# Causal short attention in a decoder kernel: first keys ahead of the row transposes, copies divided anew, a second pair of banks for the first maxima

## The reference

```python
q = (queries @ Wq.T + bq).reshape(N, L, H, -1)
k = (keys @ Wk.T + bk).reshape(N, S, H, -1)
v = (values @ Wv.T + bv).reshape(N, S, H, -1)
sm = jnp.einsum('nlhd,nshd->nlhs', q, k) / math.sqrt(D)
sm = jnp.where(triu(ones((L, S)), k=1)[None, :, None, :], -jnp.inf, sm)
attn = jnp.einsum('nlhs,nshd->nlhd', softmax(sm), v)
return attn.reshape(N, L, H * D) @ Wo.T + bo
```

## Time and profile before

| | us |
|---|---|
| median of 3 runs | 1110.2 (1110.14 to 1110.24) |
| span of the profiled execution | 1106.3 |
| time of the profiled execution beside its span | not listed; the runs' median lies 3.9 above it |
| PE busy in the span | 899.7 (81%) |
| VectorE busy | 741.0 (67%) |
| ScalarE busy | 583.1 (53%) |
| GpSimd busy | 242.7 (22%) |
| causal attention stage, first PE instruction to that of the next stage | 456.5 to 543.6 |

### The profile page before, as it was taken

How to read it: one execution, slowest core, us unless ns; L and a number is a source line. 1 busy time by engine, 2 the same in 40 slices (tenths; PEclk the granted TensorE clock), 3 DMA queues, 4 the chain that set the end, 5 groups by cost and what they waited for, 6 DMA issues and landing times. The chain is left out here.

```text
span 1106.3 us, 18228 instructions
## 1 busy us (share of the span) xinstructions
PE 899.7 (81%) x6163; PEld 555.5 (50%) x6163; DVE 741.0 (67%) x2036; ACT 583.1 (53%) x1770; POOL 242.7 (22%) x356
## 2 busy tenths in 40 slices
PE   6997999999795462679766799794777999999997
PEld 3446999998463130425543377373672233333333
DVE  6568777877573896446576644623557888898863
ACT  5785777777323200413454434452353777777784
POOL 4004455554100113202120000322501111111110
PEclk9599999999897685658876899796795899999999
DMA  9600000000004500000001000562122011111000
GB/s 231 153 19 1 2 1 2 2 1 2 1 1 57 62 0 15 16 0 2 1 1 54 1 1 1 165 170 56 21 41 67 1 27 27 27 27 21 2 1 15
DMA packets 76185, 35.81 MB, mean 32 GB/s; under 512 B 35236, under 2 KB 74572, under 8 KB 76093
## 3 DMA queue, kind: packets, MB, share of 16 engines
q1 hardware_dynamic: 73724, 33.61, 13.7%
q0 software_dynamic: 896, 0.63, 0.2%
q10 hardware_dynamic: 1472, 0.41, 0.2%
HBM read 24.42 MB, written 11.05 MB: 32 GB/s over the span
## 5 line engine op out<-in xcount | busy, mean ns | idle before, releaser
L493 DVE TENSOR_REDUCE L3x_NMP<-L3x_pM 128x1 f32<-128x361 f32 x384 | 178.2, 524 | 20.0 <-PE L3x_pM L726 19.2
L647 ACT ACTIVATE L3x_E<-L3x_pS 128x400 f32<-128x400 f32 (+1 forms) x375 | 164.5, 509 | 47.3 <-PE L3x_pS L750 46.3
L726 PE MATMUL L3x_pM<-ctx_tm 64*128 64x361 bf16 x384 | 103.6, 340 | 14.0 <-DVE L3x_NMP L493 9.7
L750 PE MATMUL L3x_pS<-ctx_tm 64*128 64x400 bf16 (+1 forms) x375 | 105.5, 350 | 1.6 <-POOL ctx_tm L437 1.2
L1787 ACT ACTIVATE L0x_E<-L0x_E,ctx_r 128x100 f32<-128x100 f32 x288 | 105.1, 369 | 0.5 <-DVE L0x_E L1667 0.5
L767 PE MATMUL L3x_pO<-L3x_E,CT 128*32 128x400 f32 (+1 forms) x768 | 85.1, 515 | 0.6 <-ACT L3x_E L647 0.4
L726 PEld LDWEIGHTS L3x_pM<-ctx_tm 64*128 64x128 bf16 x384 | 30.2, 96 | 109.5 <-DVE L3x_NMP L493 90.4
L1913 PE MATMUL L0x_pU<-ctx_tm,L0x_E 128*100 128x129 f32 x576 | 67.8, 273 | 1.1 <-POOL L0x_E L1596 1.1
L1596 POOL TENSOR_TENSOR L0x_E<-L0x_E,L0x_RZ 128x1200 f32<-128x1200 f32 x24 | 52.6, 2193 | 72.3 <-DVE L0x_RZ L1692 72.3
L1901 PE MATMUL L0x_pS<-L0x_QS,CT 128*128 128x100 f32 x576 | 68.4, 275 | 0.0
L1901 PEld LDWEIGHTS L0x_pS<-L0x_QS,CT 128*128 128x128 f32 x576 | 66.2, 192 | 0.4 <-ACT L0x_QS L1779 0.4
(11 more groups left out here) (681 smaller groups left out, 2120.6 us busy)
## 6 DMA issues: line engine op xcount, KB each, us to landing
ctx_tm<-in_ctx SPq DMA_DIRECT2D x8, 704.0 KB
ctx_tm<-key_terms SPq DMA_DIRECT2D x16, 270.8 KB, 4.3
key_terms<-ctx_tm SPq DMA_DIRECT2D x42, 90.2 KB
ctx_tm<-in_L_ffn_wi SPq DMA_DIRECT2D x4, 512.0 KB, 7.5
ctx_tm<-in_L_ffn_wo SPq DMA_DIRECT2D x4, 512.0 KB
ctx_tm<-query_terms SPq DMA_DIRECT2D x16, 75.0 KB, 3.6
slots_in<-L2a_zeros SPq DMA_DIRECT2D x8, 129.0 KB
L2f_XS<-slots_in SPq DMA_DIRECT2D x4, 258.0 KB, 3.0
```

Source lines behind the costliest of these rows:

```text
L493: nc.vector.tensor_reduce(NMP[:, p, i // NC4, a, i % NC4:i % NC4 + 1], v, AX.X, ALU.max, negate=True).then_inc(s_mr, 1)
L647: nc.scalar.activation(E[0:r, n % EB, :], score_bank(n)[0:r, 0:NG * T], ACT.Exp, scale=SCALE8).then_inc(s_e, 1)
L726: nc.tensor.matmul(pM[:, n % 3, 0:CW], key_rows(QS, a)[:, b, p, 128 * x:128 * x + 128], key_rows(KS, a)[:, b % KB, c, p, :], start=True, s ...
L750: nc.tensor.matmul(score_bank(n)[0:NW[k], 0:NG * T], key_rows(KS, a)[:, b % KB, k % 4, p, 128 * (k // 4):128 * (k // 4) + NW[k]], key_rows ...
```

## The change

- PE's start: the key product of the first half goes ahead of `ln_tensor`; then come the transposes, the first half's query product and the second half's key product. The value products move behind `max_scores(0)` and the second half's query product behind `max_scores(1)`.
- Copies: the first half's four masked key copies go from ACT to DVE (`keys_by_vector`); the first half's plain query copy and all five of the second half go from DVE to ACT (`queries`), masked with a second table of masked biases, bgq, which POOL makes.
- Banks: units 2, 4 and 6 put their maxima's scores into pO instead of pM (`max_banks`); units 2 to 7 wait for one reduction less (`reader_before`). Unit 2 waits for the values to be read out of pO, `weigh(0)` for seven reductions.
- Two semaphores, s_kv and s_qa, count the moved copies. The non-causal call keeps its order.

```diff
-def ln_tensor(nc, pe, m, q, banks, src=None):
+def ln_tensor(nc, pe, m, q, banks, src=None, rows=range(B)):
 
     src = m.XN if src is None else src
-    for b in range(B):
+    for b in rows:
...
+            bgq = s.sb("bgq", [128, NG])
...
+        if causal:
+            s_kv, s_qa = s.sem("keys_by_vector"), s.sem("queries_by_scalar")
...
+        BY_ACT = 0 if causal else NG
...
+        def in_out_banks(u):
+            return causal and u in (2, 4, 6)
+
+        def max_banks(u):
+            return pO if in_out_banks(u) else pM
+
+        def reader_before(u):
+            if in_out_banks(u):
+                return u - 1
+            return u - 1 if causal and 3 <= u <= 7 else u
...
+                    nc.gpsimd.tensor_tensor(bgq[:, :], m.gmask[:, :], bias[0][:, 0:1].broadcast_to((128, NG)),
...
                 def query(h, i):
                     if i == 0:
                         dve.wait_ge(s_q, h + 1)
+                    elif causal:
+                        dve.wait_ge(s_qa, 1)
...
-                    if i == 0 and causal:
-                        nc.vector.tensor_scalar(QN[:, c], src, bias[0][:, 0:1], None, ALU.add).then_inc(s_qs, 1)
-                    elif i == 0:
+                    if i == 0:
...
+                def keys_by_vector():
+                    dve.wait_ge(s_bg, 1)
+                    dve.wait_ge(s_k, 1)
+                    for g in range(BY_ACT, NG):
+                        nc.vector.tensor_scalar(KB[:, g, 0:HALF], pX[:, 0:HALF], m.gmask[:, g:g + 1], bg[:, g:g + 1],
+                                                ALU.mult, ALU.add).then_inc(s_kv, 1)
...
-                                            pM[0:T, :, 0:NG * T].rearrange("t a (g k) -> t a g k", k=T),
+                                            max_banks(u)[0:T, :, 0:NG * T].rearrange("t a (g k) -> t a g k", k=T),
...
-                for i in range(NQ):
+                if causal:
+                    keys_by_vector()
+                for i in range(1 if causal else 0, NQ):
                     query(0, i)
...
-                        for i in range(NQ):
-                            query(1, i)
+                        if not causal:
+                            for i in range(NQ):
+                                query(1, i)
...
+                def queries(h, lo, hi):
+                    act.wait_ge(s_q, h + 1)
+                    c, src = slice(h * HALF, (h + 1) * HALF), pS[:, h, 0:HALF]
+                    for i in range(lo, hi):
+                        if i == 0:
+                            nc.scalar.activation(QN[:, c], src, ACT.Identity, bias=bias[0][:, 0:1]).then_inc(s_qa, 1)
+                        else:
+                            nc.scalar.activation(QB[:, i - 1, c], src, ACT.Identity, bias=bgq[:, i - 1:i],
+                                                 scale=m.gmask[:, i - 1:i]).then_inc(s_qa, 1)
...
-                    for g in range(NG):
+                    for g in range(BY_ACT if h == 0 else NG):
...
+                    if causal and h == 0:
+                        act.wait_ge(s_kv, NG)
...
+                if causal:
+                    queries(0, 0, 1)
                 key(0)
                 key(1)
+                if causal:
+                    queries(1, 0, NQ)
...
+                def key_product(h):
+                    if causal:
+                        pe.wait_ge(s_cxs, h + 1)
+                    else:
+                        pe.wait_ge(q.xTs, h + 1)
+                    nc.tensor.matmul((pX, pP)[h][:, 0:HALF], wT[:, 1, :],
+                                     (CX if causal else m.XNT)[:, h * HALF:(h + 1) * HALF],
+                                     start=True, stop=True).then_inc(s_k, 1)
+
+                def query_product_of(h):
+                    pe.wait_ge(q.xTs, h + 1)
+                    nc.tensor.matmul(pS[:, h, 0:HALF], wT[:, 0, :], m.XNT[:, h * HALF:(h + 1) * HALF],
+                                     start=True, stop=True).then_inc(s_q, 1)
+
+                def value_products():
+                    for b in range(B):
+                        src = (CX if causal else m.XNT)[:, b * T:(b + 1) * T]
+                        out = pO[0:T, b // HB, (b % HB) * D:(b % HB + 1) * D] if causal \
+                            else pO[0:T, 0, b * KD:(b + 1) * KD]
+                        last = nc.tensor.matmul(out, src, wT[:, 2, 0:KD], start=True, stop=True)
+                    last.then_inc(s_v, 1)
...
+                    pe.wait_ge(s_w, 1)
+                    key_product(0)
+                    ln_tensor(nc, pe, m, q, [pS[:, 0, :], pS[:, 1, :]])
+                    query_product_of(0)
+                    key_product(1)
+                else:
+                    ln_tensor(nc, pe, m, q, [pS[:, 0, :], pS[:, 1, :]])
+                    pe.wait_ge(s_w, 1)
+                    query_product_of(0)
+                    key_product(0)
+                    key_product(1)
+                    query_product_of(1)
+                    value_products()
...
                     b, p = u // 2, u % 2
+                    bank = max_banks(u)
                     if u == 0:
-                        pe.wait_ge(s_ks, NG)
-                        pe.wait_ge(s_qs, 1)
+                        if causal:
+                            pe.wait_ge(s_kv, NG)
+                            pe.wait_ge(s_qa, 1)
+                        else:
+                            pe.wait_ge(s_ks, NG)
+                            pe.wait_ge(s_qs, 1)
                     elif u == 2 * HB:
-                        pe.wait_ge(s_ks, NQ + NG)
-                        pe.wait_ge(s_qs, NQ + 1)
+                        pe.wait_ge(s_ks, BY_ACT + 1 + NG)
+                        if causal:
+                            pe.wait_ge(s_qa, 2)
+                        else:
+                            pe.wait_ge(s_qs, NQ + 1)
+                    if u == 2 and causal:
+                        pe.wait_ge(s_vs, 1)
                     if u >= 1:
-                        pe.wait_ge(s_mr, u)
+                        pe.wait_ge(s_mr, reader_before(u))
...
-                            nc.tensor.matmul(pM[0:T, a, 0:NG * T], m.ident16[0:T, 0:T], mask16[:, 0, :],
+                            nc.tensor.matmul(bank[0:T, a, 0:NG * T], m.ident16[0:T, 0:T], mask16[:, 0, :],
...
-                        nc.tensor.matmul(pM[0:T, a, 0:NG * T], group_rows(QN, j)[:, tokens(b)],
+                        nc.tensor.matmul(bank[0:T, a, 0:NG * T], group_rows(QN, j)[:, tokens(b)],
...
-                        pe.wait_ge(s_ks, NQ)
+                        pe.wait_ge(s_ks, BY_ACT + 1)
...
-                        pe.wait_ge(s_qs, 2 * NQ)
-                        pe.wait_ge(s_ks, 2 * NQ)
+                        pe.wait_ge(s_qs, NG if causal else 2 * NQ)
+                        if causal:
+                            pe.wait_ge(s_qa, 1 + NQ)
+                        pe.wait_ge(s_ks, BY_ACT + NG + 2)
...
                     if b == 0:
                         pe.wait_ge(s_vs, 1)
+                        if causal:
+                            pe.wait_ge(s_mr, 7)
...
+                    if causal and t == 0:
+                        value_products()
+                    if causal and t == 1:
+                        query_product_of(1)
```

More of the change, by code:

```diff
@@ L988, in _ @@
                     nc.gpsimd.tensor_tensor(bg[:, :], m.gmask[:, :], bias[1][:, 0:1].broadcast_to((128, NG)),
+                                            ALU.mult)
+                    nc.gpsimd.tensor_tensor(bgq[:, :], m.gmask[:, :], bias[0][:, 0:1].broadcast_to((128, NG)),
                                             ALU.mult).then_inc(s_bg, 1)
@@ L1308, in _ @@
                             last.then_inc(s_cx, 1)
-                ln_tensor(nc, pe, m, q, [pS[:, 0, :], pS[:, 1, :]])
-                pe.wait_ge(s_w, 1)
-                if causal:
-                    pe.wait_ge(s_cxs, 2)
-                    nc.tensor.matmul(pX[:, 0:HALF], wT[:, 1, :], CX[:, 0:HALF], start=True, stop=True)\
-                      .then_inc(s_k, 1)
-                    nc.tensor.matmul(pP[:, 0:HALF], wT[:, 1, :], CX[:, HALF:TOK], start=True, stop=True)\
-                      .then_inc(s_k, 1)
@@ L1317, in _ @@
-                pe.wait_ge(q.xTs, 1)
-                nc.tensor.matmul(pS[:, 0, 0:HALF], wT[:, 0, :], m.XNT[:, 0:HALF], start=True, stop=True)\
-                  .then_inc(s_q, 1)
-                if not causal:
-                    nc.tensor.matmul(pX[:, 0:HALF], wT[:, 1, :], m.XNT[:, 0:HALF], start=True, stop=True)\
-                      .then_inc(s_k, 1)
-                pe.wait_ge(q.xTs, 2)
-                if not causal:
-                    nc.tensor.matmul(pP[:, 0:HALF], wT[:, 1, :], m.XNT[:, HALF:TOK], start=True, stop=True)\
-                      .then_inc(s_k, 1)
@@ L1327, in _ @@
-                nc.tensor.matmul(pS[:, 1, 0:HALF], wT[:, 0, :], m.XNT[:, HALF:TOK], start=True, stop=True)\
-                  .then_inc(s_q, 1)
-                for b in range(B):
```

(6 more changed lines are left out.)

## The result

The changed kernel takes **1093.9 us** (median of 4 runs, 1092.19 to 1095.93) against 1110.2 of the kernel before: ratio 0.9861, 95% interval 0.9844 to 0.9877. It is faster, as forecast. The time is 3.4 us above the predicted 1090.5 and inside the range of 1087 to 1098.

A forecast was written before the change was run, and what follows sets the result against it. It took an alternating chain in the causal stage, no engine full, at half clock for 34.1 us, as the bound. 19.5 + 0.3 less 0.1 turns span 1106.3 into 1086.6; plus 3.9 gives 1090.5 us, range 1087 to 1098.

The forecast's parts named there:

- Step 1: Causal stage's start: key product ahead of the transposes, four masked key copies on DVE, 2.49 us, done at 463.3.
- Step 2: Eight row transposes queue behind the key product: 1.4 us taken, bounds 0.95 and 2.22; ACT's plain query copy ends 464.2.
- Step 3: First products of the causal stage: first reduction starts at 466.7 instead of 468.46, 1.8 us gained.
- Steps 4 and 5: Query copies leave DVE, second bank pair for ticks 1 to 7: 4.5 us gained at reduction 1, 8.6 at reduction 3.
- Step 6: Scores and exponentials bind next: exponential 0 at 475.6, exponential 4 at 485.0; 19.5 us gained, between 17.3 and 20.7.
- Step 7: Rest of the causal stage: same instructions at full clock, about 0.3 us less; added waits cost 0.1.
- The clock: PE's granted clock stays 1.00 throughout steps 5 and 6; forecast with later stages within 3 us, chance 0.72.
- The first rival: Clock falls anyway near 471 in the causal stage: gain 9.9 us, time 1100.3, or 1094 to 1102; chance 0.14.
- the second rival: Stages behind the causal one give back 4 to 8 us through shifted low-clock stretches: 1094 to 1098; chance 0.09.
- the term of 3.9: Whole program: median of the runs, 1110.2, lies 3.9 us above the profiled span, added to the predicted span of 1086.6.
- clock stays down to the end: Clock doesn't rise again in the causal stage, so the kernel is slower than before: 1115 us; chance 0.03.
- chain not shortened: ACT's five query copies make score 0 late and first ticks only queue: 1108 to 1111 us; chance 0.02.

The follow-up runs named there:

- the three delays: Changed kernel with two, four or eight extra copies out of PSUM at the end of DVE's causal-stage work: 1090.2, 1090.8 and 1093.9 us.
- the idle products two stages on: Changed kernel plus twelve unread 128 x 128 PE products in the fixed-keys stage, two stages behind the causal one: 1088.6 us.
- the three with a part undone: Changed kernel with one pair of banks, PE's old start order, or the old division of copies, one at a time: 1099.6, 1099.1 and 1098.7 us.
- The repeated kernel: Changed kernel, nothing edited, timed again in more runs: 1090.1 us, ratio 0.9817 to the kernel before.
- the kernel with idle products: Kernel before the change plus unread 128 x 400 PE products behind ticks 1 to 8 of the causal stage: 1100.4 us.

## Why the prediction was right, and where it wasn't

The stage began 0.4 us sooner than in the kernel before (456.13 for 456.51), so a step that took just what was said stands 0.4 earlier than its predicted time.

- **Step 1**, keys by DVE from 460.8 and 2.49 long: 460.36 and 2.50. Right; nothing else wanted DVE.
- **Step 2**, eight queued transposes at the low clock, taken at 1.4 between 0.95 and 2.22: 1.54. ACT's plain query copy ended at 463.92 for the predicted 464.2.
- **Step 3**, first reduction at 466.7: 466.36, right to 0.1 when counted from the stage's start. It came at 10.05 to 10.24 from the start in all six profiled executions that have the whole change (the two of the changed kernel, the three delays, the idle products two stages on).
- **Steps 4 and 5**, reductions 1, 2 and 3 at 469.2, 471.1 and 472.3: 468.86, 470.92 and 472.24.
- **Step 6** is where the stage's 1.0 us was lost. Exponential 0 at 475.6: 475.84, which is 0.6 late from the stage's start. The split was in time (done at 474.19 for 474.3), but the turn behind it ran at 475.07 only: PE was still in the products of tick 5 and of score 0, which the prediction left out there. Four rounds to exponential 4 in 9.4, bounds 8.2 and 11.6: 9.84, another 0.4. The gain at exponential 4 is then 18.8 on the profile's scale (485.68 for 504.47) where 19.5 was said, and 18.4 counted from the stage's start.

```profile
475.07 0.35 PE L1429 MATMUL L1x_pX<-ident,L1x_MXP 100*128 100x100 bf16 x4
```

- **Step 7**: 38.70 us from exponential 4 to the next stage, 39.09 before: 0.4 for the 0.3. ACT's query copies ended at 472.6 and the first copy of the maxima came at 472.48, as said; exponential 0 didn't wait for them.
- **The clock**, 0.72 for 1.00 throughout: right, and by the reason that it gave, no idle time over 0.4 between the ticks. All six profiled executions with the whole change keep 1.00 from the first rise to the last exponential, and the kernel before and the three with a part undone do not. The first rival's fall near 471 is what each undone part then showed: 471.7, 467.7, 473.2.
- **Later stages**: the forecast had them unchanged within 3 us, the second rival 4 to 8 longer. In the profiled execution they are 4.9 longer, so there the rival came, at its low end, and so did the sign that the prediction set for it: the span is 1092.1, 5.5 off the predicted 1086.6, where over 3 was to speak for it. The span falls by 0.4 (ahead of the stage) + 18.8 - 4.9 = 14.3, from 1106.3 to 1092.1 within rounding. The price it put on a microsecond at low clock was also near: 21 us more at 0.50 in the next four went with 5.9 us more, 0.28 each, where it had allowed up to 0.42.
- **Around the span**: the term of 3.9 was wrong as a term. In the changed kernel's profiled execution it is 1.8 (1093.9 less 1092.1), and in every run on record that lists its span, those of the kernel before among them, it is 1.75 to 1.87. So the profiled execution before took about 1108.1, and 2.1 of the 3.9 was that it lay below the median. The same kernel's medians were 1107.0 to 1109.1 with the experiments, with runs from 1105.0 to 1112.4: a change of 2.2 us, which the prediction took as measurable, is no more than these medians differ among themselves.
- **The other rivals** (clock stays down to the end, chain not shortened) found nothing for them.

The 3.4 us over the forecast are thus, by the profiled execution, 1.0 of the stage (19.8 said, 18.8 measured), less 0.4 ahead of it, 4.9 of the stages behind and less 2.1 around the span. The step that failed is the last line of the sum, which carried nothing for the stages behind, and the 3.9 beside it hid part of that. The mechanism in the stage is borne out; that the time still fell inside 1087 to 1094, by 0.1, is luck, since a loss of 4.9 and a term 2.1 too large partly offset each other. The repeated kernel's 1090.1 lies closer to the predicted 1090.5, but against a kernel before of 1109.1. Whether the 4.9 us are typical of the changed kernel is only half settled. The two profiles of it show the same long set, but the second was of the slowest of its five runs (1092.82; the others 1084.63 to 1090.60). And over the eleven rows of the table, the gain of the median less the gain in the stage lies between -2.7 and 2.8, with four below -0.5 and five above 0.5: on the whole the gain in the stage arrives in the time. What decides the draw in a given run wasn't found.

On what lowers the clock the rows now say more than the prediction had. In the stage each fall to 0.50 between ticks followed a gap on PE: 1.12, 1.12 and 2.85 us in the three undone kernels, and the changed one has none of 0.3 us or more from 463.4 up to 503. The Trainium skill, "TensorE: Matmul & The Clock Gate", section "HAM oscillation — how this bites in real kernels", names idle time between bursts as the cause, in a kernel that waits 3 to 5 us for data. The trace agrees on the direction, with far shorter gaps. A gap alone is not enough, though. In the changed kernel's second feed-forward stage behind this one a gap of 1.91 us stood between products 128 rows high, and the clock stayed at 1.00:

```profile
692.08:743.28 51.20, 43.23 (x328) 33.65 (x327) 14.55 (x39) 27.04 (x64) 20.98 (x22) 1.00 0.49 123
```

```profile
699.41 0.55 PE L3163 MATMUL L2f_pU<-ident,L2f_values_turned 128*128 128x128 f32 x3 [1.91 <-issue]
```

What raises it again stays open. In two kernels PE was busy 23.74 of 23.9 us and stayed at 0.50, with no gap over 0.2 us to blame. Its work there was mostly scores 32 rows high (15.8 us in the kernel with the old PE order), then masks 100 rows high (6.3). The height of the products suggests itself: the rises at 495.6 and 497.1, that at 505.1 before, and the one at 472.25 in the kernel with idle products all came while products 128 rows high ran. But it is not shown. With the old PE order the clock rose at 491.55, ahead of the first such product at 491.96, and the changed kernel ran the same narrow ticks from 469.5 to 482 at 1.00 and kept it. No run varied the height alone.

## What to carry to other kernels

A stage of short alternating products has two costs, the chain and the clock that goes down behind the chain's gaps; here they were at most 11.0 and at least 7.8 us of 18.8. So price a removed wait with its clock, expect parts that each close one of several gaps not to add up, and, before reordering anything, test the clock's share with idle products into an unread bank in the gaps. A stage's gain is read in the stage: the stages behind it, though nothing in them was changed, differed by up to 7.5 us between profiled executions, and one profile of them says little.

## What the runs showed of the hardware

- Gaps of 1.12, 1.12 and 2.85 us on PE between narrow products stood ahead of 23.9 us at half clock in three different kernels (23.89, 23.90 and 23.89), in two of which PE was busy all but 0.16 us of them. The fall came 0.8 to 1.8 us behind the end of the gap. I had expected full occupation by itself to count for more.
- Useful work can be the filler: the 16 value products (1.99 us at the full clock), moved under the wait for reduction 0, fill the place where the kernel with the old PE order has its 1.12 us gap and then its fall.
- The same four stages, with the same instructions, took 224.3 to 231.8 us in eleven profiled executions, and two of them took one of a few lengths (35.7 to 36.3 or 38.7 to 38.8 for fixed keys; 67.1 to 67.7 or 69.8 for the wide attention), longer where more of them was at 0.50. The causal stage itself repeated to 0.2 us (68.25, 68.26, 68.08).
